# A ring of four image pairs in SBUF instead of eight, in a 3x3 convolution with group normalisation

## The reference

```python
bw = cw + jax.lax.stop_gradient(jnp.sign(W) - cw)      # the sign of W
g = v.reshape(B_, G, C_ // G, H_, W_)                  # _gn: G = 32, eps = 1e-05
m = jnp.mean(g, axis=(2, 3, 4), keepdims=True)
s = jnp.var(g, axis=(2, 3, 4), keepdims=True)
return ((g - m) / jnp.sqrt(s + eps)).reshape(v.shape)
...
x = x + _L0_conv_ref(_gn(x), L0_conv_W)                # 3x3, stride 1, padding 1
```

## Time and profile before

| | us |
|---|---|
| median of 3 runs | 206.25 |
| lowest and highest of the 3 | 205.93, 206.54 |
| the profiled execution, its own time | 206.47 |
| span of the profiled execution, first to last instruction | 204.7 |
| mean granted TensorE clock | 1.000 |

### The profile page before, as it was taken

One profiled execution on the slowest core, in us unless ns is written; L12 is line 12 of the kernel. 1 busy time (PEld: TensorE's weight loads), 2 busy tenths in 40 slices (PEclk: granted clock), 3 DMA queues, 4 the chain that ended last, 5 costly groups with the idle time before them and its releaser, 6 DMA issues.

```text
span 204.7 us, 10453 instructions
## 1 busy us (share of the span) xinstructions
PE 196.7 (96%) x4782; PEld 165.3 (81%) x4782; DVE 149.0 (73%) x320; ACT 138.5 (68%) x177; POOL 134.8 (66%) x86
## 2 busy tenths in 40 slices
PE   1999999999999999999999999999999999999993
PEld 0686978878899999989788787978788797878873
DVE  1894997976949496794949689594958859460955
ACT  3295969588593949769394976939496794939500
POOL 1059596939586793958578495858859585875900
PEclk9999999999999999999999999999999999999999
DMA  6949788887969788796979879697887969442464
GB/s 209 313 152 303 202 335 278 259 298 210 351 180 378 235 275 286 220 382 164 366 218 294 284 231 365 144 387 205 307 283 261 304 172 370 181 160 95 154 230 160
DMA packets 19116, 52.20 MB, mean 255 GB/s; under 512 B 2112, under 2 KB 4928, under 8 KB 19072
## 3 DMA queue, kind: packets, MB, share of 16 engines
q1 hardware_dynamic: 19072, 51.54, 74.9%
HBM read 25.84 MB, written 25.69 MB: 252 GB/s over the span
## 4 chain that ended last, share of the span: by engine, by line
PE 92%; DMA 3%; DVE 2%; SPq 1%; ACT 0%; issue 0%; DVEq 0%
PE psum L513 91%; DMA w_raw<-in_L_conv_W_dram 3%; DVE xbuf L466 2%; SPq L155 1%; PE psum L487 1%; ACT w_sign L290 0%; PE psum L497 0%; DVEq L56 0%
## 5 line engine op out<-in xcount | busy, mean ns | idle before, releaser
L236 POOL TENSOR_TENSOR los<-xnorm,his 128x840 f16<-128x840 f32 (+1 forms) x64 | 105.9, 1686 | 26.4 <-ACT his L274 15.8
L513 PE MATMUL psum<-los,w_taps 64*64 64x392 f16 (+1 forms) x2268 | 110.5, 325 | 0.0
L513 PE MATMUL psum<-his,w_taps 64*64 64x392 f16 x2268 | 110.2, 325 | 0.0
L513 PEld LDWEIGHTS psum<-his,w_taps 64*64 64x64 f16 x2268 | 81.9, 107 | 15.8 <-issue 0.4
L513 PEld LDWEIGHTS psum<-los,w_taps 64*64 64x64 f16 x2268 | 84.1, 107 | 13.0 <-POOL los L236 0.6
L388 DVE SCALAR_TENSOR_TENSOR xbuf<-psum,xbuf 128x784 f32<-128x784 f32 (+1 forms) x60 | 58.1, 969 | 40.8 <-PE psum L513 39.9
L339 DVE BATCH_NORM_STATS2 stats<-xbuf 128x6 f32<-128x448 f32 x112 | 64.0, 614 | 4.4 <-DMA xbuf<-in_x_dram 3.9
L266 ACT ACTIVATE xnorm<-xbuf,coef 128x784 f32<-128x784 f32 (+2 forms) x62 | 62.7, 1035 | 1.4 <-DVE coef L371 1.0
L274 ACT CAST his<-xnorm 128x784 f16<-128x784 f32 (+2 forms) x62 | 50.2, 835 | 0.3 <-issue 0.2
L242 POOL TENSOR_TENSOR xbuf<-moved,xbuf 128x784 f32<-128x784 f32 x15 | 27.9, 1863 | 32.9 <-ACT moved L283 32.9
L282 ACT ACTIVATE moved<-psum 64x784 f32<-64x784 f32 x15 | 12.3, 820 | 44.2 <-PE psum L513 44.2
(11 more groups left out here) (26 smaller groups left out, 21.8 us busy)
## 6 DMA issues: line engine op xcount, KB each, us to landing
out_dram<-xbuf SPq DMA_DIRECT2D x63, 392.0 KB, 4.7
xbuf<-in_x_dram SPq DMA_DIRECT2D x47, 448.0 KB, 4.4
xbuf<-in_x_dram SPq DMA_DIRECT2D x18, 224.0 KB, 4.9
out_dram<-xbuf SPq DMA_DIRECT2D x1, 224.0 KB, 2.2
out_dram<-xbuf SPq DMA_DIRECT2D x2, 84.0 KB, 1.8
w_raw<-in_L_conv_W_dram SPq DMA_DIRECT2D x1, 144.0 KB, 5.3
```

What stands on the lines that cost most here:

```text
L236: nc.gpsimd.tensor_tensor(rows(los[:, pair % HRING, :], a, b), rows(xnorm[:, pair % NRING, :], a, b), rows(his[:, pair % HRING, :], a, b), ...
L513: mm = pe.matmul(outs[:, a - n * BR:b - n * BR, left:right], w_taps[lanes, t, :], rows(half[lanes, slot, :], a + dy, b + dy)[:, :, left + ...
```

## The change

The ring has four slots instead of eight. `XRING` also sets the sizes of `xbuf` (from 8 to 4 slots of 12,544 bytes per partition) and of `coef`, the numbers of the semaphores `loaded` (32 to 16) and `stored` (16 to 8), and the values that are waited for.

```diff
@@ -15,7 +15,7 @@
 
 SCALE = 2.0 ** 9
 
-XRING = 8
+XRING = 4
 HRING = 3
 NRING = 2
 WARM_UP = (14, 6, 1)
```

## The result

The changed kernel took 210.5 us (median of 4 runs, 209.45 to 211.79) against 206.39 us before (4 runs, 205.93 to 206.8). The ratio is 1.0205, with a 95% interval of 1.0172 to 1.0238. It is slower by about 2%; the forecast was no change, and the range ended at 207.1 us. The profiled execution took 211.44 us, its span is 209.7 us, 5.0 us longer than before.

What follows compares the result with a forecast made beforehand. TensorE was taken to bound the kernel, with loads early enough. All terms summed to 0 on the path, so the forecast was 206.25 us, the median itself, with a range of 205.6 to 207.1 us.

Steps and rivals of the forecast that it cites:

- the clock: Rival on TensorE: late loads idle it, it falls from 2.4 to 1.2 GHz; one such pair makes 218 us; chance 0.01.
- the end: Last store's wait on SyncE, 0.8 us: fewer slot waits shorten nothing; outside the span 0, bounded at 0.3 us either way.
- What stands behind the wait on SyncE: SyncE's queue after part 0: part 1 follows at 116.9 us, part 2 and next store not held, part 3 in time; cost 0.
- Part 0: Pair 11's first load waits for the store, 3.7 us later, lands at 121.3 us, 0.8 us before its reader; cost 0.
- the first step of this sequence: On SyncE, part 0 of pair 11 is issued 3.7 us later, at 116.5 us, when the store lands.
- the backlog: DMA queue ahead of part 3, from later parts 0 and 1: nothing added, bound +1.1 us, cost 0.
- its longest case for part 1: Part 1 on SyncE's queue with longest legs: issued at 118.6 us, landed at 124.4 us, 0.6 us late for its reader.
- its middle case: Part 1 on SyncE's queue: issued about 116.9 us, 4.8 us and about one more, landed at 122.7 us; reader at 123.84 us.
- the charge in full: Lost lead of part 0 charged in all 12 pairs at 3.7 us: 45 us, making 251 us; the prediction took 0.
- no new wait of its own: Sign on TensorE that the forecast holds: pair starts still 11.82 us apart, without a new wait of TensorE.
- The rival I gave 0.08: Slower: store, load and statistics close into a loop; 4.4 us, 210.7 us, or milder 207 to 208 us; chance 0.08.
- Its loop: Store of pair p, statistics of p + 4, coefficients of p + 3: 35.5 us over three pairs, 3.9 us free.

Runs made afterwards that it cites:

- e7: Changed kernel with its four slots and waits, but each first-half store DMA writes 98 columns instead of 784: 206.04 us, ratio 0.9983.
- e6: Kernel before, eight slots, loads one pair further ahead; from pair 7 part 0 waits for the same store as in the changed kernel: 210.36 us.
- e5: Kernel before, eight slots, no wait on a near store; loads one pair further ahead, three parts in a burst, then part 3: 214.14 us, ratio 1.0401.
- a0_changed_again: The changed kernel once more, unaltered, on another chip than its first runs: 211.9 us.
- e2_late_no_store_wait: Kernel before, eight slots, no wait on a near store; parts 0 and 1 of pairs 4 to 15 issued late, in one burst with part 2: 214.06 us.
- e4_five_slots: Kernel before with five slots instead of eight; part 0 waits for the store of the pair five ahead: 206.19 us, ratio 0.9987.
- e8_four_slots_capped: Changed kernel, but each load or store DMA first waits for the landing of the DMA three before it: 214.58 us.
- e10_burst_early_capped: Kernel of e5, but each load or store DMA first waits for the landing of the DMA three before it: 206.25 us, ratio 1.0.
- e11: Changed kernel with parts 0 and 1 each waiting for one store half, and a limit of three DMAs under way: median 210.34 us of 12 runs.

## Why the prediction was wrong

**What held.** TensorE sets the pace where nothing stops it, the clock stayed full, and the end is as it was. A part 0 that is late by 1.5 to 3.7 us is harmless (e7), and this is what the prediction had worked out from the traces of the single DMAs.

**The step that failed** is "What stands behind the wait on SyncE": "The later parts 0 and 1 could leave a backlog there. But ... I add nothing", and "Part 2 and the next store come a phase later and are not held"; with it the legs of "Part 0", where I took 5.4 and 4.8 us "from the very DMAs that move. If anything it is high". The time from the issue of a DMA to its landing depends on what else is queued at that moment, and the change moves the queue: the medians went from 4.7 to 6.5 us for stores and from 4.5 to 5.4 us for loads. Part 0 late means parts 1 and 2 no longer ahead of the stores but on top of them; the store lands later; the next part 0 waits for it. Parts 0 of pairs 4 and 15 are issued at 33.0 and 172.7 us in the changed kernel, 12.7 us apart on average over eleven pairs, against 11.8 us for TensorE. The prediction had computed the first step of this sequence, 3.7 us, and stopped, where the lateness grew to 12.7 us. It put the backlog at 0, and the backlog is what costs the time: 4.1 us in e6 and 7.9 us in e5, with no datum late, in stops of TensorE that no engine ends (below).

What was missing is a sum over a whole round. A pair moves 3.2 MB. In the changed kernel the DMA engines move 360 GB/s between 112 and 120.25 us, where they are full, which makes 8.9 us; the stretch in which the awaited landing leaves them nearly empty is 3.1 us on average. Together that is 12.0 us, already more than TensorE's 11.8 us. The bytes and the rate were in the trace before; the length of the empty stretch was not, as no load waited for a landing there.

Smaller slips of the prediction: its longest case for part 1 (issued at 118.6, landed at 124.4 us) leaves out the "about one more" us of its middle case, and 12 x 3.7 is 44.4, so that the charge in full would be 250.7 and not 251 us. Nothing rests on either. Of its signs of being wrong the main one was missing: "no new wait of its own" was looked for in waits for `los`, `his` and `coef`, not in stops that no releaser ends.

**The rival I gave 0.08** has the right time, 210.7 us, for largely the wrong reason, which is luck. Its loop needs late data, and e6 shows the same 210.4 us with data a pair early. In the trace of a0_changed_again every wait of the weight loads from 20 to 195 us is without a releaser:

```profile
PEld psum L513 <- issue: 7.3, 10, 1.5
```

In the first profile of the changed kernel both are there, 3.2 us without a releaser and 3.6 us through VectorE and GpSimd, and its span is 5.0 us longer. (The waits of the weight loads add up to more than the span gained, those of the matmuls, 3.0 us, to less: in the example below the weight loads stop for 0.88 us and the matmuls for 0.49 us.) So there late data did stop TensorE, and in a0 they did not, although statistics waited 14.2 us for loads in it. How the loss splits between the two differs from run to run. That the late data make the total larger isn't shown: the span of a0 is 5.7 us longer than before, without any such stop.

**What was not in the prediction at all** is the third user of the DMA engines, the instructions. The page of before had it in its list of queues, and I passed over it because its share is small:

```profile
q8 instruction: 37, 0.61, 1.3%
```

How close to the edge it stood can be worked out from the trace: the time from the weight load at which TensorE enters a block of 256 instructions (the places of the gaps fix where blocks begin) to the start of the packet that brings the next block, for the blocks entered between 50 and 175 us. A block lasts 5.3 us, the packet itself takes about 1 us.

| kernel | blocks | median start us | latest start us | over 2.95 us | of these with a gap |
|---|---|---|---|---|---|
| before | 24 | 1.4 | 3.3 | 2 | 1 |
| changed, first profile | 23 | 1.9 | 4.1 | 6 | 5 |
| changed, a0 | 23 | 2.6 | 4.3 | 9 | 9 |
| e2_late_no_store_wait | 22 | 2.8 | 4.7 | 8 | 8 |
| e5_burst_early | 22 | 3.0 | 4.8 | 13 | 11 |
| e6_early_with_wait | 23 | 2.3 | 4.2 | 7 | 7 |
| e4_five_slots | 24 | 1.2 | 2.6 | 0 | 0 |
| e7_small_first_store | 24 | 0.5 | 2.5 | 0 | 0 |
| e8_four_slots_capped | 22 | 0.6 | 2.7 | 0 | 0 |
| e10_burst_early_capped | 24 | 0.6 | 2.9 | 0 | 0 |

Over all fourteen traces these are 323 blocks. In 257 the packet started within 2.95 us of the entry, and in none of them did a gap over 0.15 us without a releaser follow at the next block; in 66 it started later, and in 58 of them one did. After a gap TensorE goes on 1.2 to 1.7 us after the packet's end. For example, in the changed kernel one block is entered at 74.0 us, the next block's packet starts at 78.1 us and ends at 79.1 us, and this is what the weight loads then do:

```profile
78.11 1.32 PEld L513 LDWEIGHTS psum<-los,w_taps 64*64 64x64 f16 x31
80.31 0.13 PEld L513 LDWEIGHTS psum<-los,w_taps 64*64 64x64 f16 x5 [0.88 <-issue]
```

They run dry at 79.4 us, in the middle of 36, and go on at 80.31 us. In the kernel before, the same block was entered at 74.1 us and the packet started at 76.3 us, and there was no gap. The Trainium skill (Runtime: NRT & Kernel Launch, Instruction fetch mechanics) says that instructions come in blocks of 16 KiB with 256 instructions, over a DMA queue of the sequencer's own, and that this is mostly hidden. The blocks and the queue agree with this trace, 37 packets of 16,384 bytes and gaps at multiples of 256 instructions. That it is hidden holds here only while the data queue is short; with it full, it cost 4.1 us (e6) to 7.9 us (e5).

That DMAs under way cause the gaps is shown, by e5 against e10. That the packets are what TensorE waits for is inferred, from the fixed places of the gaps and the packets' times; no row names them as releaser. Any other cause would have to strike at every 256th instruction as well, and just when a packet is late.

**Open.** Why the four-slot kernels vary by several us from run to run, and what the high runs of e11 do, which the limit on the queue did not remove. The split of the loss in the changed kernel between instructions and late data.

## What to carry to other kernels

When a change ties a load to the landing of a store, do not take the legs from the old trace: work out the whole round of the queue, bytes over rate plus the stretch in which each awaited landing leaves it empty, and compare it with the pace of the engine that bounds. Of a wait added to a queue that is written out by hand, ask what the things behind it become; a burst of DMAs can stop an engine that waits for none of them, here by all signs because its instructions come over the same DMA engines, and the mark of it is a gap with no releaser, at multiples of 256 instructions (128 weight loads). Here a ring of five slots saves three of the four slots that the change saves, at no cost, since the store it waits for was issued a pair earlier.

## What the hardware showed that was not expected

- A kernel whose data are all early lost 8 us (e5) when its DMAs of some 400 KB came in bursts, up to seven under way, and got it back when a wait before each kept them at four or less (e10).
- A 16 KB instruction packet takes about 1 us. It starts 0.6 us (median) after TensorE enters the block before it when at most four data DMAs are under way (e10), and 3.0 us (median) to 4.8 us after it in the bursts of e5; over 2.95 us, TensorE stops in 58 of 66 cases over all traces, and below that in none of 257.
- At the end of a store the DMA engines' share was 0.06 for 2 us (120.25 to 122.25 us in the changed kernel), as if one of the 16 ran on alone, and a wait for the landing pays for it.
